# Ranks and places right after the division, product masks ahead of the choice of experts, in the fused attention and routing stage

## What is computed

```
qkv = concatenate([qkv, agg])                 # agg: depthwise 5x5, then grouped 1x1
q, k = relu(q), relu(k);  v = concatenate([v, ones])
vk = einsum('bhds,bhes->bhde', v, k)
out = einsum('bhde,bhes->bhds', vk, q)
out = out[:, :, :-1] / (out[:, :, -1:] + EPS)
x = x + batchnorm(conv1x1(out, w_proj))
t = tokens of x;  t = layernorm(t)
x_norm = layernorm(t) * g + b
logits = x_norm @ gate_w
dispatch_w, expert_idx = top_k(softmax(logits), 2)
out += combine[:, e] * (gelu(x_norm @ w1[e] + b1[e]) @ w2[e] + b2[e])   # for each expert e
```

## Time and profile before

| | us |
|---|---|
| median of 3 runs | 2451.37 |
| lowest and highest run | 2450.63, 2451.95 |
| the profiled execution | 2458.47 |
| its span, first to last instruction | 2456.7 |

### The profile page before, as it was taken

One profiled execution on the slowest core, in us unless ns is written; L12 is line 12 of the kernel. 1 busy time (PEld: TensorE's weight loads), 2 busy tenths in 40 slices (PEclk: granted clock), 3 DMA queues, 4 the chain that ended last, 5 costly groups with the idle time before them and its releaser, 6 DMA issues. The chain is left out here.

```text
span 2456.7 us, 44417 instructions
## 1 busy us (share of the span) xinstructions
PE 2023.7 (82%) x13648; PEld 1119.6 (46%) x13649; DVE 1440.9 (59%) x3119; ACT 1130.6 (46%) x1707; POOL 647.5 (26%) x669
## 2 busy tenths in 40 slices
PE   5839999999999999978649995996678871299994
PEld 2411223222232222145438884564456541299993
DVE  4849888887887886044426666652245454044444
ACT  4620576675766767822224441541134341144443
POOL 1240010000100001037745562000002444455551
PEclk9865899999999999976669996999989775599996
DMA  3474142222422220032223334102011311233226
GB/s 131 158 193 69 30 51 46 44 27 45 52 46 45 27 44 2 1 101 84 72 82 104 106 103 154 77 35 68 25 35 35 110 47 51 70 90 91 87 78 215
DMA packets 113504, 180.17 MB, mean 73 GB/s; under 512 B 23296, under 2 KB 66560, under 8 KB 111040
## 3 DMA queue, kind: packets, MB, share of 16 engines
q1 hardware_dynamic: 94912, 138.22, 23.0%
q0 software_dynamic: 18432, 39.88, 4.7%
HBM read 99.02 MB, written 69.01 MB: 68 GB/s over the span
## 5 line engine op out<-in xcount | busy, mean ns | idle before, releaser
L552 DVE TENSOR_REDUCE mx<-bank 128x1 f32<-128x512 f32 x1024 | 633.4, 681 | 121.6 <-PE bank L434 121.5
L537 ACT ACTIVATE P<-bank 128x1024 f32<-128x1024 f32 x512 | 496.0, 1021 | 323.9 <-PE bank L486 323.4
L434 PE MATMUL bank<-ks,qs 96*128 96x512 bf16 x1024 | 368.8, 412 | 34.9 <-DMA ks<-qk_parts 30.2
L1223 POOL DMA_INDIRECT results<-yo,places x284 | 274.4, 966 | 255.8 <-DVE yo L1213 209.2
L486 PE MATMUL bank<-qs,ks 99*128 99x512 bf16 x1024 | 307.8, 385 | 9.7 <-issue 5.3
L1139 PE MATMUL bank<-xt,up 128*128 128x256 f32 x1136 | 282.8, 393 | 9.0 <-ACT up L1162 1.6
L466 PE MATMUL bank<-P,vt 128*32 128x512 f32 x2048 | 274.5, 608 | 0.7 <-ACT P L537 0.7
L2230 POOL DMA_INDIRECT dispatched<-planes,places x128 | 125.4, 980 | 499.2 <-DVE places L2167 382.6
L1139 PEld LDWEIGHTS bank<-xt,up 128*128 128x128 f32 x1136 | 209.0, 194 | 46.0 <-issue 19.0
L434 PEld LDWEIGHTS bank<-ks,qs 96*128 96x128 bf16 x1024 | 100.3, 98 | 271.9 <-DVE mx L552 158.6
L486 PEld LDWEIGHTS bank<-qs,ks 99*128 99x128 bf16 x1024 | 77.4, 97 | 291.4 <-ACT P L537 204.1
(11 more groups left out here) (285 smaller groups left out, 2640.0 us busy)
## 6 DMA issues: line engine op xcount, KB each, us to landing
xr<-dispatched SPq DMA_DIRECT2D x142, 130.0 KB, 2.2
y<-results SPq DMA_DIRECT2D x64, 256.0 KB, 4.3
qk_parts<-parts SPq DMA_DIRECT2D x16, 768.0 KB, 4.8
qs<-qk_parts SPq DMA_DIRECT2D x96, 128.0 KB
ks<-qk_parts SPq DMA_DIRECT2D x96, 128.0 KB
v_turned<-vt SPq DMA_DIRECT2D x8, 1024.0 KB, 3.9
vt<-v_turned SPq DMA_DIRECT2D x8, 1024.0 KB
src<-e_to_fold SPq DMA_DIRECT2D x8, 643.0 KB, 4.2
```

Source lines behind the costliest of these rows:

```text
L434: pe.matmul(bank[:, slot, :], qs[0:KB, par, h, c * C:(c + 1) * C], ks[0:KB, par, h, half * HALF:(half + 1) * HALF], start=True, stop=True) ...
L537: act.activation(P[:, x % SLOTS, :], bank[:, 2 * pair:2 * pair + 2, :] .rearrange("p a t -> p (a t)"), ACT.Exp).then_inc(probs_ready, 1)
L552: dve.tensor_reduce(mx[:, k // 2, k % 2:k % 2 + 1], bank[:, slot, :], AX.X, ALU.max).then_inc(unit_freed, 1)
L1223: pool.indirect_dma_start(yd_dram, bass.IndirectOffsetOnAxis(places[:, p, q:q + 1], 0), yo[:, p, q, :], None).then_inc(sent[p], 16)
```

## The change

Nothing is added and nothing removed; three things change their place.

1. PE issues `ranks(b-3)` right after `fractions(b-1)`, ahead of `turn`, `mix` and `logits`; the list `order` has it there too, so that the rotation of banks changes.
2. DVE runs `locate(b-3)` right after `divide(b-1)`, ahead of `moments(b-2)`. Before, it followed `choose(b-2)`.
3. DVE runs `mask_products(b)` ahead of `choose(b-2)`, behind `residual(b-2)`; `add(b-1)` stays last.

```
@@ -1706,13 +1706,13 @@
     for b in range(B + 3):
         if 1 <= b <= B:
             order += [(what, b - 1, i) for i in range(4) for what in ("num", "den")]
+        if b >= 3:
+            order.append(("ranks", b - 3))
         if b < B:
             order += [("ka", b, n) for n in range(2)] + [("va", b, n) for n in range(2)]
             order += [("qa", b, n) for n in range(2)]
         if 2 <= b < B + 2:
             order.append(("logits", b - 2))
-        if b >= 3:
-            order.append(("ranks", b - 3))
@@ -1903,14 +1903,14 @@
                 if 1 <= b <= B:
                     fractions(b - 1)
+                if b >= 3:
+                    ranks(b - 3)
                 if 2 <= b < B + 2:
                     turn(b - 2)
                 if b < B:
                     mix(b)
                 if 2 <= b < B + 2:
                     logits(b - 2)
-                if b >= 3:
-                    ranks(b - 3)
@@ -2171,6 +2171,8 @@
                 if 1 <= b <= B:
                     divide(b - 1)
+                if b >= 3:
+                    locate(b - 3)
                 if 2 <= b < B + 2:
                     moments(b - 2)
@@ -2178,11 +2180,10 @@
                 if 2 <= b < B + 2:
                     affine(b - 2)
                     residual(b - 2)
-                    choose(b - 2)
-                if b >= 3:
-                    locate(b - 3)
                 if b < B:
                     mask_products(b)
+                if 2 <= b < B + 2:
+                    choose(b - 2)
                 if 1 <= b <= B:
                     add(b - 1)
```

## The result

The changed kernel takes 2384.8 us, the median of four runs (2381.37 to 2387.18), against 2451.66 us (2450.63 to 2452.18, four runs) of the kernel before: a ratio of 0.9727, 95% interval 0.971 to 0.9744. That is 66.9 us less. The forecast was 2370 with a range of 2361 to 2384, so the direction and the cutting of POOL's ring came as told, and the time lies 0.8 us above the upper end. The profiled execution took 2383.84 us, with a span of 2382.0.

A forecast was written before the change was run, and what follows sets the result against it. A ring of POOL, ACT and DVE (33.85 us) bounds the stage; cut, burst 0 at 1863.2, burst 1 at 1885.9, 3 x 23, 20.7 per later burst and 3.7 end at 2041.4: 82 us less, 2369, said 2370, range 2361 to 2384.

The forecast's parts named there:

- POOL's ring: Landing of a burst, `normalize`, choice, `locate`, next burst: 33.85 us per burst, to be cut by the earlier places.
- Burst 0: POOL's first burst of the changed stage: start at 1863.2 instead of 1878.2, after the last division, `locate` and 0.8.
- I take 23: Iteration of the changed stage, spacing of bursts 1 to 4: 23 us, from 22.8 and 22.2 plus small waits.
- my ends of 20.7 and 24.9: Bounds for an iteration: 20.7 us with POOL itself the bound, 24.9 with the clock granted at 0.86 on average.
- the loop through DVE and ACT: Chain through DVE, PE and ACT from one start of the choice to the next: 22.8 us.
- 22.2 for PE alone: PE's own iteration without a wait, busy throughout at a granted clock of 1.00: 22.2 us.
- a slack of only 0.5 against the logits: Choice ahead of burst 1: `locate` delays the chain by 1.8 us, of which 0.5 was slack against the logits.
- The rotation of banks, I price this at nothing: PE's bank order with `ranks` earlier: `qa`'s wait covered, third fraction waiting for the choice's first instruction; no cost.
- a rival at 0.09: Cold PE: gaps of 2 to 4 us, partly 1.2 GHz, iterations 27 to 30 us, 2381 to 2390; chance 0.09.
- The median of the runs is 7.1 us below it.: Profiled execution of the kernel before, 2458.5 us, against its median; the 7.1 us were taken off the forecast too.
- the wait covered with 2 us to spare: DVE's masks ahead of the choice wait for `vk`, full about two us before the residual is done.
- the stretched sends: POOL's sends over 1.0 us beside DVE's choice: sign of the mild rival, about 2418 us, chance 0.05.

The follow-up runs named there:

- `kT` first: Changed kernel with ACT copying `kT` ahead of the two `rs`: 2374.99 us in one run, ratio 0.9686 to the kernel before.
- the two other remedies: On the changed kernel with `kT` ahead of `rs`: products interleaved with logits, `locate` behind the moments; 2376.64 us, ratio 0.9694 to the kernel before.

## Why the prediction was right, and where it failed

**The ring.** Right. The landing no longer ends `normalize`'s wait in mid-stage, the bursts come closer, and a loop of about PE's length is what comes next, as told. That the places could be had ahead of the landing carries the gain; the masks carry none that can be told (0.9753 without and 0.9727 with them, 190.2 and 190.7 us of bursts, and 1.0014 for the masks alone).

**Burst 0.** Forecast 1863.2, measured 1861.52: 1.7 us early, of which 1.2 are the stage's earlier start (its first line, L1869, at 1797.54 instead of 1798.74). The price of 1.8 for `locate` held (1858.90 to 1860.69).

**The step that failed: "I take 23" for an iteration.** It was 25.6, outside my ends of 20.7 and 24.9. Bursts 1 to 4 took 77.4 instead of 69, and burst 0 to 1 25.1 instead of 22.7; with 0.65 and 1.0 at the two steps behind, that brings the last send to 2052.2 instead of 2041.4, 10.8 us later. Two causes, the first shown by experiment, the second read from the traces:

- *Two loops taken as rivals that are one.* I added up the loop through DVE and ACT to 22.8, read 22.2 for PE alone, and took about the longer one. The iteration measured is a ring that passes through both: from the start of the last denominator through the division, `locate`, the moments, `rs` and `kT` to the logits 8.46 us (1855.85 to 1864.31), and from there on PE alone, logits, products, `project` and fractions, 16.66 (to 1880.97), together 25.12. I had moved `locate` ahead of the moments and counted its 1.8 us in the loop through DVE; that `kT`, for whose bank the logits wait, stands behind the moments on ACT, I left out of PE's 22.2, although my own sum for burst 1 names a slack of only 0.5 against the logits. It costs PE the gap of 0.93, and with the alternate 4.52 of `project` that goes with it some 1.8 us per iteration (25.6 against 23.8 with `kT` first). "The rotation of banks, I price this at nothing" was right: the logits want the bank of `kT` in both orders, and with `locate` behind the moments and the same rotation the gap is gone.
- *The clock.* I read 22.2 from two iterations that ran at 1.00 throughout. The row that spoke against it stood in my own groups, the 0.64 at 1843.3 without any gap; I used it for a rival at 0.09 instead of for the term. All six iterations now have products at about 0.5, 1.6 us more each, as three or four of six have in the kernel before. Why it is all six now isn't shown. That rival's mechanism, gaps of 2 to 4 us and fractions at 2.07, didn't occur: the fractions are pairs of 1.02 throughout.

**"The median of the runs is 7.1 us below it."** The second failed step. I carried the distance of the profiled execution from the median over to the kernel after, as if it belonged to the kernel. It belonged to one execution: the second one of before lies at 2453.25, and the profiled execution of the kernel after 1.0 below its median. And 3.9 us of it lay in the very stage that is changed (325.05 against 321.1 us), so the 82 us were reckoned from a stage that was slow in that execution. With this the account closes. The stage took 254.7 us where my sum has 242.7 (1798.74 to 2041.4), 12.0 more; with the 3.9 that is 15.9, and the measured median lies 15.8 above the 2369 of the sum. Likewise 321.1 - 254.7 = 66.4, where 66.9 were measured.

**Masks, sends, memset.** DVE did wait for `vk`, 0.66 to 0.94 us; I had called the wait covered with 2 us to spare. My own rows had less: there the choice begins at 1870.94, only 0.7 us after `project` (1870.24), and the products now take 1.6 more. The wait lies beside PE's work, since the choice isn't what PE waits for. Bursts take 20.1 to 20.4 us with choice and additions beside them, where I had taken 20.7. Sends are 0.96 with few exceptions; 9 of the 128 are over 1.0, up to 1.26, and all that they have over 0.96 comes to 1.4 us. So the stretched sends, which I had put down as a sign of being wrong, did come, but at a price that can be left out. Memset and copy came as priced, 3.4 + 0.3, and one pause of 2.83 stands in the unbroken tail.

The Trainium skill's page "SBUF — State Buffer", section "SBUF: two separate sides", would have had DVE's two-port work hold the sends up. What these traces show of it is small: a first send beside an addition was 1.42 to 1.46 before, and the two longest after, 1.25 and 1.26 at 1903.18 and 1954.36, stand beside additions (1902.31 and 1953.49) too.

## What to carry to other kernels

When an instruction is moved ahead on one engine, follow everything behind it through the other engines to the one that is to set the pace, and ask what slack it eats there; here `locate`, moved on DVE, reached PE's logits by way of the moments, `rs` and `kT`. Two loops that share a stretch are no rivals of which the longer counts: add up the ring that passes through both. A term taken from the quickest iterations of one execution is a lower bound: read all the iterations, and a second execution if there is one, before pricing the loop. The distance between a profiled execution and the median belongs to that execution, not to the kernel, and isn't carried over to the next.

## What the runs showed of the chip

- TensorE's clock fell behind the logits (sixteen matmuls of eight columns, L1887) with PE busy all along: the logits themselves run at 0.98 to 1.00 and the step behind them at 0.50 to 0.53. In the kernel before that hit three or four of the six iterations read, others in each execution; in the kernel after, all. It isn't the gap ahead of the logits, since it came without one as well (`kT` first). That the logits are the cause is argued from their place and from the products at 1.95 us in the two iterations without logits; dealing the products between them moved the spell partly to `project` (0.68) and didn't remove it, so a cause further ahead isn't excluded.
- The Trainium skill's page "TensorE: Matmul & The Clock Gate", section "What's actually happening", says that the point of transition varies from run to run, which these traces show too. Its table names idling as what throttles; here the clock fell without any idling of PE.
- One indirect send of 128 rows from POOL takes 0.96 us, and the next follows 0.30 us later; a burst of 16 takes 19.9 to 20.4 us with an iteration of DVE's work beside it (22.47 with a pause of 2.83).
- The fastest kernels measured are the changed one with `kT` ahead of `rs` on ACT, 2374.99 us in one run, and the same with the two other remedies on top of it, 2376.64 in four runs; the two can't be told apart.
